# Fourteen batched field pairs instead of ten in a pairwise-interaction kernel, with the transposes placed nearer to their use

## The chip, the cores and the metric

The kernel runs on 1 core of one Trainium2 chip. The metric is the device time of one execution in microseconds (us). Everything is float32.

## The reference

512 examples have 40 categorical fields; each field looks up a row of 64 numbers in its own table. For each of the 780 pairs of fields there is a 64x64 matrix, and the pair's number is a bilinear form. A three-layer tower follows.

```python
e = jnp.stack([tbl_0[ids[:, 0]], ..., tbl_39[ids[:, 39]]], axis=1)   # 512, 40, 64
vi, vj = x[:, i_idx, :], x[:, j_idx, :]                              # 780 pairs i < j
viW = jnp.einsum('bpd,pde->bpe', vi, W)
z = jnp.einsum('bpe,bpe->bp', viW, vj)                               # 512, 780
h = jnp.concatenate([z, dense_ctx], axis=1)                          # 512, 796
h = jnp.maximum(h @ W_top1 + b_top1, 0.0)
h = jnp.maximum(h @ W_top2 + b_top2, 0.0)
y = h @ W_top3
```

## The kernel before, in words

Fields are taken two at a time: **field pair** k holds fields 2k and 2k+1, and the pairs come from k = 19 down to 0. Their place in that order is u = 19 - k; below, f7 means the field pair with u = 7.

A field pair passes through three engines. POOL (GpSimd) gathers its table rows with 8 indirect DMAs (`gather`, L320). PE (TensorE) turns them with four 128x128 transposes into the one PSUM bank `ps_e` (`transpose_fields`, L501). ACT (ScalarE) copies that bank into `E`, a ring of six in SBUF (`copy_fields`, L349), and then issues four DMAs (L356) that place a rearranged copy in `E4`; u = 18 and 19 have no such DMAs. The first four field pairs are made in other ways at the start.

The bilinear forms are computed in two ways.

- A **group** g is a field pair k against one quad M of four later fields (or the pairs inside a quad, M = None). It takes two **steps**. In each, PE writes two matmuls into one of three double banks of `ps_t` (`products`, L539), and DVE (VectorE) multiplies the 128x1024 result by `E` or `E4` into the ring `prod` (`multiply`, L447). Two groups are a couple. PE then sums over the partitions by matmuls with ones into `ps_z` (`reduce_two`, L561), six groups behind the products: 8 matmuls for a couple, or 4 where POOL has added the two halves beforehand (`add_halves`, L327, the groups in `ADDED`). Each chunk of 16 groups fills `ps_z` once, and DVE copies it to `z`.
- A **batched unit** B is a field pair k against the last eight fields, with the batch on the partitions. It takes four steps, one for each 128 examples: PE makes two matmuls (`batched_products`, L522), DVE multiplies by `wide_rows` into one of six buffers of the ring `batched` (`multiply_batched`, L461), and ACT sums it over 64 columns at a time, by 16 ACTIVATEs with an accumulator (`sum_batched`, L372), into `zt`. Here one call of `sum_batched` is called a **sum**; four sums belong to a batched unit, and they are numbered s1, s2, ... in order. A batched unit has no `reduce_two`.

Every engine works strictly through its own list. The lists all come from one generator, `order()`, which says where the transposes ("fields"), the groups and the batched units stand. `ahead(u)` is how many groups before its first use a field pair stands, and `BATCHED`, `BATCHED_FROM` and `BATCHED_EVERY` choose the batched pairs and their places. On ACT the four sums of a batched unit enter the list `left`, and some of the groups take one sum out of it.

The waits that matter here: PE starts step s when the product of step s - 3 is there. DVE's batched step number i (four per unit) waits until i - 5 sums are done, because of the six buffers:

```python
if at >= B_RING:
    dve.wait_ge(batched_summed, at - B_RING + 1)
```

PE's transposes into `ps_e` wait for ACT's previous copy, and groups that use a field pair wait for its copy (`e_copied`). POOL gathers f(u) only when f(u - 4) is transposed.

At the end PE turns `zt` into rows of `z` (L593), and the tower follows: L586 the first layer, L621 the second, L627 the last. The share of the first layer that needs the bank `ps_e` waits for ACT's copy of the first turned part of `zt` (L389), which stands in ACT's list behind the loop.

Weights come by one 256 KB DMA for each couple or batched unit (L289), eight ahead.

Of the kernel before, what the change touches and what calls it, by code (L numbers as in the profile page):

```python
# [25 lines left out]
PER_CHUNK = 16  # L26
# [2 lines left out]
CODE_RING = 7  # L29
G_RING = 4  # L30
E_RING = 6
W_RING = 8
P_RING = 8
B_RING = 6
STEPS = 3
LAG = 7
GATHER_LEAD = 12
PARAMS_AT = 12


# [2 lines left out]

BATCHED = (12, 10, 8, 7, 6, 5, 4, 3, 2, 1)
BATCHED_FROM, BATCHED_EVERY = 7, (13, 3)


def pair(i, j):  # L50
# [3 lines left out]
def plan_groups():  # L54
# [3 lines left out]
    for k in reversed(range(KP)):  # L58
        groups += [(k, M) for M in range(k // 2 + 1, QUADS - (WIDE // 4 if k in BATCHED else 0))]
        if k % 2 == 0:  # L60
# [6 lines left out]
NG = len(GROUPS)  # L67
NC = NG // 2
NB = len(BATCHED)
NU = NC + NB  # L70
CHUNKS = NG // PER_CHUNK
B_PAIRS = 2 * WIDE * NB
B_REST = B_PAIRS - P
ALL_CHUNKS = CHUNKS + 2
DENSE_AT = B_REST


ADDED_COUPLES = (12, 13, 15, 18, 20, 21, 23, 25, 26, 27, 28, 30, 32, 33, 34, 35, 36, 37, 38)
ADDED = [n for n in range(NG) if n // 2 in ADDED_COUPLES]


def arrival(k):
    return KP - 1 - k
# [10 lines left out]


def ahead(u):
    return 1 if u < 8 else 4


SPLIT_FIRST = (0, 2, 3, 1)  # L100
# [12 lines left out]
def order():  # L113

    u = j = units = 0
    for n in range(NG):
        while u < KP and first_group(u) - ahead(u) <= n:
            yield "fields", u
            u += 1
        yield "group", n  # L120
        if n in WIDE_AFTER:
            yield "rows", WIDE_AFTER.index(n)
        units += n % 2
        if n % 2 and j < NB and arrival(BATCHED[j]) < u and units >= (
                BATCHED_FROM + BATCHED_EVERY[0] * j // BATCHED_EVERY[1]):
            yield "batched", j
            j += 1
            units += 1
# [11 lines left out]
def last_step(u):  # L140

    k = KP - 1 - u
    return max([FIRST_STEP["group", n] + 1 for n in range(NG) for ks in pairs_of(n) if k in ks]
               + [FIRST_STEP["batched", j] + 3 for j in range(NB) if BATCHED[j] == k])

# [6 lines left out]
def tower_kernel(nc, w_units, ids, ids_by_field, tables, dense, w1, b1, w2, b2, w3, out):  # L152
    with ExitStack() as ctx:
# [20 lines left out]
        E4 = sb("E4", [P, QUADS - 1, 2, BATCH])  # L174
        w_sb = sb("w_sb", [P, W_RING, BLOCKS * P])
        prod = sb("prod", [P, P_RING, 2, 2, BATCH])
# [4 lines left out]
        small, at = {}, 0  # L181
        for f in looked_up:
            used, c = splits[f]
# [47 lines left out]
        e4_placed = [sem(f"e4_placed{u}") for u in range(KP)]  # L231
        w_loaded = [sem(f"w_loaded{i}") for i in range(W_RING)]
        step_done = sem("step_done")
        product_ready = sem("product_ready")
        halves_added = sem("halves_added")
        two_reduced = sem("two_reduced")
# [31 lines left out]
        def _(sp):  # L268
# [17 lines left out]
            def load_weights(m):  # L286
                if m >= W_RING:
                    sp.wait_ge(step_done, BLOCKS * (m - W_RING + 1))
                sp.dma_start(w_sb[:, m % W_RING, :], w_units[m]).then_inc(w_loaded[m % W_RING], 16)  # L289

            for m in range(W_RING):
                load_weights(m)
# [10 lines left out]
        def _(pool):  # L303
# [27 lines left out]
            for n in range(NG):  # L331
                while u < KP and first_group(u) <= n + GATHER_LEAD:
                    gather(u)
# [4 lines left out]
        @block.scalar  # L338
        def _(act):
            def copy_fields(u):  # L340
                k = KP - 1 - u
                if u < LOOKED_UP:
                    act.wait_ge(code_used, sum(len(codes_of) for codes_of in code_list[:u + 1]))
                else:
                    act.wait_ge(transposed, u - LOOKED_UP + 1)
                if u >= E_RING:
                    act.wait_ge(product_ready, last_step(u - E_RING) + 1)
                    act.wait_ge(e4_placed[u - E_RING], 64)
                act.activation(E[:, slot_of(k), :], e_bank[u], ACT.Copy).then_inc(e_copied, 1)  # L349
                if k < 2:  # L350
                    return
                act.wait_ge(e_copied, place(u) + 1)
                for f in range(2):
                    for h in range(2):
                        to, of = (2 * (k % 2) + f) * HALF, f * DIM + h * HALF
                        act.dma_start(E4[to:to + HALF, k // 2 - 1, h, :], E[of:of + HALF, slot_of(k), :]).then_inc(  # L356
                            e4_placed[u], 16)

            def copy_rows(u):
                at = (KP - 1 - u - WIDE_K) * 2 * DIM  # L360
                act.wait_ge(rows_turned, u + 1)
                act.activation(wide_rows[:, :, at:at + 2 * DIM], ps_e[:].rearrange("p (b n) -> p b n", b=BT),
                               ACT.Copy).then_inc(rows_copied, 1)

            def sum_batched(j, b):

                act.wait_ge(product_ready, FIRST_STEP["batched", j] + b + 1)
                for i in range(2):
                    for f in range(WIDE):
                        at = (2 * j + i) * WIDE + f  # L370
                        products = batched[:, (BT * j + b) % B_RING, i, f, :]
                        last = act.activation(products, products, ACT.Copy, accum_out=zt[:, b, at:at + 1])  # L372
                last.then_inc(batched_summed, 1)

            for u in SPLIT_FIRST:
                copy_fields(u)
            left = []
            for kind, at in order():
                if kind == "fields" and at >= FIRST:
                    copy_fields(at)  # L380
                elif kind == "rows":
                    copy_rows(at)
                elif kind == "batched":
                    left += [(at, b) for b in range(BT)]
                elif kind == "group" and left and at % 7 in (0, 2, 3, 5):
                    sum_batched(*left.pop(0))
            assert len(left) <= (B_REST // (2 * WIDE)) * BT
            act.wait_ge(zt_turned, 1)
            act.activation(z[:, CHUNKS, :], turn_bank[0], ACT.Copy).then_inc(zt_copied, 1)  # L389
            for j, b in left:  # L390
                sum_batched(j, b)
            act.wait_ge(zt_turned, 2)
            act.activation(z[0:B_REST, CHUNKS + 1, :], turn_bank[1][0:B_REST, :], ACT.Copy).then_inc(zt_copied, 1)  # L393
            act.wait_ge(params_loaded, 16 * (ALL_CHUNKS + 5))
            for m in range(H1 // P):
                act.wait_ge(h1_summed, m + 1)
                act.activation(h1[:, m, :], h1_bank[m], ACT.Relu, bias=b1_sb[:, m:m + 1]).then_inc(h1_ready, 1)
            for m in range(H2 // P):
                act.wait_ge(h2_summed, m + 1)
                act.activation(h2[:, m, :], h2_bank[m], ACT.Relu, bias=b2_sb[:, m:m + 1]).then_inc(h2_ready, 1)  # L400
            act.wait_ge(y_summed, 1)
            act.activation(y_sb[:], y_bank[0:1, :], ACT.Copy).then_inc(y_ready, 1)

        @block.vector
        def _(dve):
# [58 lines left out]
                                      ALU.mult).then_inc(product_ready, 1)  # L464

            def copy_z(c):
                dve.wait_ge(two_reduced, PER_CHUNK // 2 * (c + 1))
                dve.tensor_copy(z[:, c, :], ps_z[:]).then_inc(z_copied, 1)  # L468

            for kind, at in order():  # L470
                if kind == "batched":
                    multiply_batched(at)
                elif kind == "group":
                    multiply(at)
                    if at > LAG and at % 2 == 1 and (at - LAG + 2) % PER_CHUNK == 0:
                        copy_z((at - LAG) // PER_CHUNK)
            copy_z(CHUNKS - 1)

        @block.tensor
        def _(pe):  # L480
# [62 lines left out]
            def reduce_two(n):  # L543
                c, q = divmod(n // 2, PER_CHUNK // 2)
                if c >= 1 and q == 0:
                    pe.wait_ge(z_copied, c)
                for g in (n, n + 1):
                    pe.wait_ge(product_ready, FIRST_STEP["group", g] + 2)
                    if g in ADDED:
                        pe.wait_ge(halves_added, ADDED.index(g) + 1)  # L550
                for s in range(2):
                    for g in (n, n + 1):
                        if s == 1 and g in ADDED:
                            continue
                        if GROUPS[g][1] is None:
                            ones = halves[:, 30 - 4 * q - 2 * s:62 - 4 * q - 2 * s]
                        else:
                            ones = quads[:, 28 - 4 * q:60 - 4 * q]
                        for j in range(2):
                            to = 32 * (2 * (g % 2) + j)  # L560
                            last = pe.matmul(ps_z[to:to + 32, :], ones, prod[:, g % P_RING, s, j, :],  # L561
                                             start=(q == 0 and s == 0),
                                             stop=(q == PER_CHUNK // 2 - 1 and (s == 1 or g in ADDED)))
                last.then_inc(two_reduced, 1)

            pe.wait_ge(ident_ready, 1)
# [145 lines left out]
```

## Time and profile before

| | |
|---|---|
| median of 3 runs | 350.28 us (350.03 to 350.73) |
| the profiled execution, its own time | 350.38 us |
| its span in the trace | 348.4 us |
| PE busy | 320.4 us (92%) |
| DVE busy | 250.3 us (72%) |
| POOL busy | 228.4 us (66%) |
| ACT busy | 174.0 us (50%) |
| mean granted clock of TensorE | 0.976 |

The shares are of the span. A program's matmul appears twice in the trace (float32 takes two instructions), so a couple's 8 product matmuls are a row "x16". Matmuls overlap in the records; the time that a block takes is read from the start of one block to the start of the next, or from the chain of waits.

### The profile page before, as it was taken

What the parts mean: (1) busy time and instruction counts of PE and PEld (TensorE: products, weight loads), DVE (VectorE), ACT (ScalarE), POOL (GpSimd) and SP (SyncE); (2) the same over time, 40 slices, a digit from 0 to 9 for tenths busy, and PEclk for the clock granted to TensorE, in tenths of its full rate; (3) what the DMA queues carried; (4) which work ended last, traced back from release to release, by engine and by line L of the source; (5) the groups of instructions that cost most, each with busy time, mean ns of one, the idle gap of its engine ahead of it and who ended that gap; (6) DMA issues with size and microseconds to landing.
All of it is one profiled execution on the core that took longest, in us unless ns stands there. A gap on an engine that the chain in (4) does not pass through costs nothing.

```text
span 348.4 us, 5290 instructions
## 1 busy us (share of the span) xinstructions
PE 320.4 (92%) x1528; PEld 112.4 (32%) x1528; DVE 250.3 (72%) x252; ACT 174.0 (50%) x1312; POOL 228.4 (66%) x192
## 2 busy tenths in 40 slices
PE   0699898529999999999999999999999999999997
PEld 0133432113333333333333333333333333344432
DVE  2385696506887989799899899999998999900000
ACT  1001210000198572876947958795934999190032
POOL 6777777777777734898778884799773994700000
PEclk9999999958999999999999999999999999999969
DMA  6843453323333324933323242322221000000000
GB/s 166 250 149 94 118 131 90 79 49 87 103 95 96 88 77 131 304 83 80 101 67 87 72 109 62 84 68 64 69 66 49 0 3 0 3 0 0 0 0 0
DMA packets 17862, 27.63 MB, mean 79 GB/s; under 512 B 4901, under 2 KB 5029, under 8 KB 17834
## 3 DMA queue, kind: packets, MB, share of 16 engines
q1 hardware_dynamic: 9770, 17.86, 17.8%
q0 software_dynamic: 4608, 4.73, 6.8%
q10 hardware_dynamic: 3456, 4.72, 4.5%
q8 instruction: 12, 0.20, 0.2%
q14 instruction: 16, 0.13, 0.1%
HBM read 22.57 MB, written 0.00 MB: 65 GB/s over the span
## 4 chain that ended last, share of the span: by engine, by line
PE 73%; POOL 16%; issue 6%; DVE 3%; DMA 1%; ACT 0%; DVEq 0%
PE ps_t L539 36%; PE ps_z L561 15%; POOL rows L320 11%; PE ps_t L522 10%; PE ps_t L586 6%; POOL wide_rows L320 5%; PE ps_t L621 3%; DVE prod L447 3%; PE ps_e L501 2%; PE ps_e L586 2%; DMA rows<-in_tbl,ids_sb 1%; DMA ids_sb<-in_ids_t 1%; PE ps_t L627 1%; DVE batched L461 0%; ACT z L393 0%
## 5 line engine op out<-in xcount | busy, mean ns | idle before, releaser
L447 DVE TENSOR_TENSOR prod<-ps_t,E 128x1024 f32<-128x1024 f32 x160 | 184.7, 1217 | 35.6 <-PE ps_t L539 32.0
L372 ACT ACTIVATE batched<-batched 128x64 f32<-128x64 f32 x640 | 152.9, 241 | 23.6 <-DVE prod L447 21.1
L539 PE MATMUL ps_t<-E,w_sb 64*128 64x512 f32 x640 | 156.1, 617 | 1.0 <-DVE prod L447 0.2
L320 POOL DMA_INDIRECT rows<-in_tbl,ids_sb x128 | 121.7, 951 | 38.1 <-issue 37.6
L372 ACT ACTIVATION_READ_ACCUMULATOR batched<-batched 128x1 f32 x640 | 120.0, 188 | 0.0
L327 POOL TENSOR_TENSOR prod<-prod 128x1024 f32<-128x1024 f32 x38 | 89.0, 2371 | 30.0 <-DVE prod L447 29.9
L539 PEld LDWEIGHTS ps_t<-E,w_sb 64*128 64x128 f32 x640 | 55.9, 187 | 90.7 <-issue 60.9
L349 ACT ACTIVATE E<-ps_e 128x512 f32<-128x512 f32 x18 | 10.7, 597 | 102.4 <-PE ps_e L501 79.6
L561 PE MATMUL ps_z<-prod,quads 128*32 128x512 f32 x408 | 58.4, 600 | 0.0
L461 DVE TENSOR_TENSOR batched<-ps_t,wide_rows 128x1024 f32<-128x1024 f32 x40 | 46.2, 1218 | 5.7 <-PE ps_t L522 5.7
L522 PE MATMUL ps_t<-w_sb,E 64*128 64x512 f32 x160 | 37.3, 604 | 0.2 <-DVE batched L461 0.2
L425 DVE TENSOR_SCALAR prod<-prod,first_row_f 125x512 f32<-125x512 int32 x38 | 16.7, 500 | 12.8 <-PE ps_e L490 6.4
L490 PE MATMUL ps_e<-prod 125*64 125x512 f32 x40 | 13.4, 768 | 11.3 <-DVE prod L425 9.5
L561 PEld LDWEIGHTS ps_z<-prod,quads 128*32 128x32 f32 x408 | 11.1, 108 | 35.7 <-issue 20.4
L501 PE MATMUL ps_e<-ident,rows 128*128 128x128 f32 x64 | 10.9, 295 | 12.6 <-DMA rows<-in_tbl,ids_sb 11.8
L522 PEld LDWEIGHTS ps_t<-w_sb,E 64*128 64x128 f32 x160 | 14.2, 186 | 23.4 <-issue 15.7
L320 POOL DMA_INDIRECT wide_rows<-in_tbl,ids_sb x16 | 16.7, 1044 | 5.6 <-issue 4.6
L586 PE MATMUL ps_t<-z,w_sb 128*128 128x512 f32 (+1 forms) x42 | 19.9, 623 | 0.0
L561 PE MATMUL ps_z<-prod,halves 128*32 128x512 f32 x80 | 17.2, 598 | 0.0
L501 PEld LDWEIGHTS ps_e<-ident,rows 128*128 128x128 f32 x64 | 7.0, 145 | 24.1 <-DMA rows<-in_tbl,ids_sb 14.5
L586 PEld LDWEIGHTS ps_t<-z,w_sb 128*128 128x128 f32 (+1 forms) x42 | 7.9, 193 | 10.9 <-issue 10.9
L468 DVE COPY z<-ps_z 128x512 f32<-128x512 f32 x5 | 3.4, 683 | 10.3 <-PE ps_z L561 10.3
(41 smaller groups left out, 61.2 us busy)
## 6 DMA issues: line engine op xcount, KB each, us to landing
w_sb<-in_w_units SPq DMA_DIRECT2D x50, 256.0 KB, 2.8
E<-E ACTq DMA_DIRECT2D x72, 64.0 KB, 2.6
rows<-in_tbl,ids_sb POOLq DMA_INDIRECT x128
w_sb<-in_w SPq DMA_DIRECT2D x7, 256.0 KB
prod<-in_ids_by_field SPq DMA_DIRECT2D x2, 512.0 KB, 9.1
prod<-in_tbl SPq DMA_DIRECT2D x3, 312.5 KB
w_sb<-in_w SPq DMA_DIRECT2D x1, 512.0 KB
wide_rows<-in_tbl,ids_sb POOLq DMA_INDIRECT x16, 4.8
```

Source lines behind the costliest of these rows:

```text
L320: pool.indirect_dma_start(rows_of(u, b)[:, f * DIM:(f + 1) * DIM], None, tables[2 * k + f], bass.IndirectOffsetOnAxis(ap=ids_sb[:, col:col ...
L327: pool.tensor_tensor(prod[:, n % P_RING, 0, :, :], prod[:, n % P_RING, 0, :, :], prod[:, n % P_RING, 1, :, :], ALU.add).then_inc(halves_ad ...
L372: last = act.activation(products, products, ACT.Copy, accum_out=zt[:, b, at:at + 1])
L425: dve.tensor_scalar(codes[0:used, j % CODE_RING, :], ids_wide[0:used, i, :], float(c), first_row_f[0:used, i:i + 1], ALU.subtract, ALU.is_ ...
L447: dve.tensor_tensor(prod[:, n % P_RING, s, :, :], ps_t[:, step % STEPS, :, :], multiplier, ALU.mult).then_inc(product_ready, 1)
L461: dve.tensor_tensor(batched[:, at % B_RING, :, :, :].rearrange("p i f n -> p i (f n)"), ps_t[:, step % STEPS, :, :], wide_rows[:, b, None, ...
L490: pe.matmul(e_bank[u][half:half + DIM, :], small[f][:, c, :], codes[0:splits[f][0], j % CODE_RING, :], start=(c == 0), stop=(c == splits[f ...
L501: last = pe.transpose(e_bank[u][:, b * P:(b + 1) * P], rows_of(u, b), ident[:])
L522: last = pe.matmul(ps_t[:, step % STEPS, i, :], E[at:at + DIM, slot_of(k), b * P:(b + 1) * P], w_sb[at:at + DIM, m % W_RING, :], start=Tru ...
L539: last = pe.matmul(ps_t[:, step % STEPS, j, :], w_sb[at:at + DIM, m % W_RING, col:col + P], E[at:at + DIM, slot_of(pairs_of(n)[s][j]), :], ...
L561: last = pe.matmul(ps_z[to:to + 32, :], ones, prod[:, g % P_RING, s, j, :], start=(q == 0 and s == 0), stop=(q == PER_CHUNK // 2 - 1 and ( ...
L586: last = pe.matmul(h1_bank[m], w1_sb[0:used, c, m * P:(m + 1) * P], z[0:used, c, :], start=(c == 0), stop=(c == ALL_CHUNKS - 1))
```

## The change

There are 14 batched units (k = 14, 12, 11, ..., 0) instead of 10. Each takes two groups away, so there are 72 groups instead of 80, and 50 units in all as before: 36 couples and 14 batched units, instead of 40 and 10. Their places are written out in `BATCHED_AT`, counted in units. 38 groups are still halved by POOL. The transposes stand 1 group ahead (u < 12) or 2 groups, instead of 1 (u < 8) or 4. POOL gathers 14 groups ahead instead of 12. The ring of weights has 6 places instead of 8. On ACT every group takes out a sum while any is left, instead of four groups in seven. `zt` has 224 columns instead of 160, so that the second part turned at the end has 96 rows instead of 32.

```diff
-W_RING = 8
+W_RING = 6
-GATHER_LEAD = 12
+GATHER_LEAD = 14
...
-BATCHED = (12, 10, 8, 7, 6, 5, 4, 3, 2, 1)
-BATCHED_FROM, BATCHED_EVERY = 7, (13, 3)
+BATCHED = (14, 12, 11, 10, 9, 8, 7, 6, 5, 4, 3, 2, 1, 0)
+BATCHED_AT = (4, 6, 9, 11, 14, 17, 21, 24, 28, 31, 35, 38, 42, 45)
...
-CHUNKS = NG // PER_CHUNK
+CHUNKS = -(-NG // PER_CHUNK)
...
-ADDED_COUPLES = (12, 13, 15, 18, 20, 21, 23, 25, 26, 27, 28, 30, 32, 33, 34, 35, 36, 37, 38)
+ADDED_COUPLES = (12, 13, 15, 17, 18, 19, 20, 22, 23, 24, 25, 26, 27, 29, 30, 31, 32, 33, 34)
...
 def ahead(u):
-    return 1 if u < 8 else 4
+    return 1 if u < 12 else 2
...
-        if n % 2 and j < NB and arrival(BATCHED[j]) < u and units >= (
-                BATCHED_FROM + BATCHED_EVERY[0] * j // BATCHED_EVERY[1]):
+        if n % 2 and j < NB and arrival(BATCHED[j]) < u and units >= BATCHED_AT[j]:
             yield "batched", j
...
-                elif kind == "group" and left and at % 7 in (0, 2, 3, 5):
+                elif kind == "group" and left:
                     sum_batched(*left.pop(0))
...
-                dve.wait_ge(two_reduced, PER_CHUNK // 2 * (c + 1))
+                dve.wait_ge(two_reduced, min(PER_CHUNK // 2 * (c + 1), NC))
...
-                                             stop=(q == PER_CHUNK // 2 - 1 and (s == 1 or g in ADDED)))
+                                             stop=((q == PER_CHUNK // 2 - 1 or n == NG - 2)
+                                                   and (s == 1 or g in ADDED)))
```

With the change the middle of the program reads as follows (sums in brackets where ACT's list has them, B0 the first batched unit): g7, B0, g8 [s1], f7, g9 [s2], B1, g10 [s3], f8, g11 [s4], g12 [s5], f9, g13 [s6], B2, g14 [s7], g15 [s8], B3, f10, g16 to g18 [s9 to s11], f11, g19 [s12], B4, g20, g21 [s13, s14], f12, g22, g23 [s15, s16], B5, g24, g25 [s17, s18], f13, and so on; later f14 stands behind s23, f15 behind s28, f16 behind s34, f17 behind s40, f18 behind s45 and f19 behind s50 of 56.

**ACT's list, from the copy of f8 on.** L349 (after: L348) is the copy of a field pair, L356 (L355) its four DMAs, L372 (L371) the sums, 16 ACTIVATEs each. Before:

```order
L349 ACTIVATE E<-ps_e 128x512
L356 DMA E<-E 32x512 x4
L349 ACTIVATE E<-ps_e 128x512
L356 DMA E<-E 32x512 x4
L372 ACTIVATE batched,zt<-batched 128x64 x32
L349 ACTIVATE E<-ps_e 128x512
L356 DMA E<-E 32x512 x4
L372 ACTIVATE batched,zt<-batched 128x64 x48
L349 ACTIVATE E<-ps_e 128x512
L356 DMA E<-E 32x512 x4
```

Now, from the same copy of f8 on:

```order
L348 ACTIVATE E<-ps_e 128x512
L355 DMA E<-E 32x512 x4
L371 ACTIVATE batched,zt<-batched 128x64 x32
L348 ACTIVATE E<-ps_e 128x512
L355 DMA E<-E 32x512 x4
L371 ACTIVATE batched,zt<-batched 128x64 x48
L348 ACTIVATE E<-ps_e 128x512
L355 DMA E<-E 32x512 x4
L371 ACTIVATE batched,zt<-batched 128x64 x48
L348 ACTIVATE E<-ps_e 128x512
L355 DMA E<-E 32x512 x4
```

Sums now stand between the copies of f8 and f9, where none stood, and three instead of two between f9 and f10; by f11 ACT's list has 11 sums behind it instead of 5.

**PE's list, from the transposes of f12 (L501, after: L500) to those of f13.** L539 (L538) are a group's products, 4 matmuls each, L522 (L521) a batched unit, L561 (L560) `reduce_two`. Before:

```order
L501 MATMUL ps_e<-ident,rows 128x128 x4
L539 MATMUL ps_t<-E,w_sb 128x512 x8
L561 MATMUL ps_z<-prod,halves 32x512 x2
L561 MATMUL ps_z<-prod,quads 32x512 x2
L561 MATMUL ps_z<-prod,halves 32x512 x2
L561 MATMUL ps_z<-prod,quads 32x512 x2
L539 MATMUL ps_t<-E,w_sb 128x512 x8
L561 MATMUL ps_z<-prod,quads 32x512 x8
L501 MATMUL ps_e<-ident,rows 128x128 x4
```

Now:

```order
L500 MATMUL ps_e<-ident,rows 128x128 x4
L538 MATMUL ps_t<-E,w_sb 128x512 x8
L560 MATMUL ps_z<-prod,halves 32x512 x2
L560 MATMUL ps_z<-prod,quads 32x512 x2
L560 MATMUL ps_z<-prod,halves 32x512 x2
L560 MATMUL ps_z<-prod,quads 32x512 x2
L521 MATMUL ps_t<-w_sb,E 128x512 x8
L538 MATMUL ps_t<-E,w_sb 128x512 x8
L560 MATMUL ps_z<-prod,quads 32x512 x8
L500 MATMUL ps_e<-ident,rows 128x128 x4
```

A batched unit (B5) now stands between the two, so f13 can be turned only when B5 and the couple behind it are through.

## Rows read from the trace of the kernel before

**Rows 1.** The page: busy time of each engine; PE, ACT, granted clock in 40 slices.

```profile
PE 320.4 (92%) x1528; PEld 112.4 (32%) x1528; DVE 250.3 (72%) x252; ACT 174.0 (50%) x1312; POOL 228.4 (66%) x192
...
PEclk9999999958999999999999999999999999999969
```

**Rows 2.** The chain that ended last, in order of time: start us, us, what.

```profile
73.91 2.37 DMA rows<-in_tbl,ids_sb
76.32 1.12 PE ps_e L501 x4
77.44 3.31 PE ps_t L539 x8
80.75 1.85 PE ps_z L561 x16
82.60 3.63 PE ps_t L539 x16
...
91.72 0.59 PE ps_e L501 x4
...
150.98 1.00 PE ps_z L561 x8
...
289.15 2.17 PE ps_t L539 x8
291.42 2.17 PE ps_t L539 x8
...
304.70 0.59 PE ps_e L593 x4
...
318.83 5.15 PE ps_e L586 x12
```

**Rows 3.** Busy time by stretch, between f8's arrival and the loop's end.

```profile
76.30:302.90 226.60, 225.63 (x1180) 78.04 (x1184) 204.86 (x181) 153.25 (x1228) 171.21 (x125) 0.99 0.29 79
```

**Rows 4.** PE in order of time, around the arrivals of f6, f7 and f8.

```profile
56.98 0.66 PE L501 MATMUL ps_e<-ident,rows 128*128 128x128 f32 x4 [1.18 <-DMA rows<-in_tbl,ids_sb]
...
66.45 0.66 PE L501 MATMUL ps_e<-ident,rows 128*128 128x128 f32 x4 [1.41 <-DMA rows<-in_tbl,ids_sb]
76.32 1.12 PE L501 MATMUL ps_e<-ident,rows 128*128 128x128 f32 x4 [9.21 <-DMA rows<-in_tbl,ids_sb]
```

**Rows 5.** POOL in order of time: two of the 80 gathers in a row.

```profile
70.17 0.94 POOL L320 DMA_INDIRECT rows<-in_tbl,ids_sb  x1 [0.30 <-issue]
71.41 0.95 POOL L320 DMA_INDIRECT rows<-in_tbl,ids_sb  x1 [0.30 <-issue]
```

**Rows 6.** ACT in order of time, two sums (the first 16 ACTIVATEs start 95.46) and a copy.

```profile
95.46 0.26 ACT L372 ACTIVATE batched<-batched 128x64 f32<-128x64 f32 x1 [2.52 <-DVE prod L447]
...
103.12 0.58 ACT L349 ACTIVATE E<-ps_e 128x512 f32<-128x512 f32 x1
103.73 2.44 ACTq L356 DMA_DIRECT2D E<-E  x4
106.22 0.26 ACT L372 ACTIVATE batched<-batched 128x64 f32<-128x64 f32 x1 [2.52 <-issue]
...
117.61 0.18 ACT L372 ACTIVATION_READ_ACCUMULATOR batched<-batched 128x1 f32 x1
```

**Rows 7.** DVE in order of time, twelve steps in a row.

```profile
42.49 13.67 DVE L447 TENSOR_TENSOR prod<-ps_t,E 128x1024 f32<-128x1024 f32 x12 [1.85 <-DMA E<-E]
```

**Rows 8.** Groups of instructions: DVE's steps, and the two halves of ACT's sums.

```profile
L447 DVE TENSOR_TENSOR prod<-ps_t,E 128x1024 f32<-128x1024 f32 x160 | 184.7, 1217 | 35.6 <-PE ps_t L539 32.0 <-DMA E<-E 1.9 <-issue 1.4
L372 ACT ACTIVATE batched<-batched 128x64 f32<-128x64 f32 x640 | 152.9, 241 | 23.6 <-DVE prod L447 21.1 <-issue 2.5
L372 ACT ACTIVATION_READ_ACCUMULATOR batched<-batched 128x1 f32 x640 | 120.0, 188 | 0.0
```

**Rows 9.** Stretches after PE's last work at 67.1: PE busy first, granted clock third from right.

```profile
66.00:68.00 2.00, 0.66 (x4) 0.42 (x4) 0.66 (x1) 0.60 (x1) 1.39 (x3) 1.00 0.07 16
68.00:70.00 2.00, 0.00 (x0) 0.00 (x0) 0.00 (x0) 0.00 (x0) 1.56 (x2) 0.99 0.42 96
70.00:72.00 2.00, 0.00 (x0) 0.00 (x0) 0.00 (x0) 0.00 (x0) 1.53 (x2) 0.50 0.40 97
...
80.00:81.00 1.00, 1.00 (x8) 0.16 (x8) 0.99 (x2) 0.00 (x0) 0.85 (x1) 0.89 0.52 141
```

**Rows 10.** DMA issues on the page: the weights, us from issue to landing.

```profile
w_sb<-in_w_units SPq DMA_DIRECT2D x50, 256.0 KB, 2.8
```

## The prediction

> **What bounds the kernel now.** I read the page first: PE is busy 92% of the span, ACT 50% [rows 1]. Then the chain of waits: it runs over POOL's gathers until f8's rows land, and from 76.32 almost only over PE [rows 2]. Between there and the end of the loop PE is busy 225.6 of 226.6 us, DVE 204.9, ACT 153.3 [rows 3]. So the kernel has two parts: a front paced by gathers, 1.248 us each, 10.0 us for a field pair [rows 5], and a loop paced by PE.
>
> PE's prices, from the chain [rows 2]: a couple's products or a batched unit 3.63 us (a group 1.82), a full `reduce_two` 1.85, a halved one 1.00, four transposes 0.59. After a batched unit a couple takes 2.17 + 2.17 = 4.34, 0.7 more, since DVE's steps come every 1.14 us (13.67 over 12) and PE's every 0.91 [rows 7]; a DVE step by itself is 1.22 [rows 8].
>
> ACT's prices: two sums from 95.46 to 103.12 are 3.83 each, three from 106.22 to about 117.8 are 3.86. I take 3.86. A copy with its DMAs takes 3.10 (103.12 to 106.22), in which ACT sums nothing [rows 6]. A copy without DMAs is 0.6, as the ACTIVATE alone.
>
> **The change on PE.** Four couples become four batched units. Their products cost the same; four full reductions go, 4 x 1.85 = 7.4 us. Also, before f8 there are now two batched units (7.3 us) in place of one couple's tail, so PE is no longer waiting at 76.3. It would wait for f9 instead, 10.0 us later, at 86.3. From f9 on the work is that of before from f8 on, less 0.59 (f8), less ten groups (18.2), plus two batched units (7.3), less five full reductions (9.25): 20.8 less. 10.0 later with 20.8 less work gives -10.8; the slow clock at f8 is gone too (1.12 + 3.31 against 0.59 + 1.82, 2.0 us [rows 2]). **By PE alone the time would be 350.4 - 12.8 = 337.6.**
>
> **The change on ACT.** 16 more sums, 56 in all. ACT's list is serial: 56 x 3.86 = 216.2, copies of f7 to f17 11 x 3.10 = 34.1, f18 and f19 1.2, together 251.5 us behind the first sum's start. That start: f6 lands at 56.98 [rows 4]; now g6 and g7 are behind it. PE will have idled some 7 us there, so I charge the slow clock: transposes 1.12, a group 3.31, a group 1.82, the reduction 1.85, B0's first step 0.91, DVE 1.22 and 0.1 between: 67.3. ACT therefore ends its sums at 318.8 at the earliest, without one wait. Behind them are its copy 0.6 and, from 318.83 to the end, 29.6 us of tail, plus 2.0 outside the span: **351 us is a floor** (349 with the first clock at full). ACT, half idle before, takes away all the gain by itself.
>
> It costs more than the floor, because ACT's lag is passed on through the ring of six. The fourth step of B(j) waits for s(4j - 2): that of B5 for s18. And the transposes stand only one or two groups ahead, so where f(u) comes soon behind B(j), ACT comes to its copy while PE is still held by that very sum. Call T the end of that sum.
>
> - f12 and f13 stand right behind it. From T: DVE 1.25, PE one step 0.91, the next waits for DVE's product (2.4) and ends at 3.4, reduction 1.85, transposes 0.59: ACT waits 5.8 us, twice.
> - f11: the same plus a group (1.82), less s11 (3.86): 3.7. f10: B3 is in between, 9.4 less two sums: 1.7.
> - Before, none of this exists: sums stand four groups in seven and the transposes four groups ahead.
>
> Together 17.0 us. From f14 on the transposes are done before ACT comes (s23, s28 and so on, each one or more sums behind T). Then f17: ACT starts its copy at 67.3 + 40 x 3.86 + 10 x 3.10 + 17.0 = 269.7, while PE has finished B10 at about 264. PE waits; g50 starts at 270.4. From there PE has 22 groups 40.0, three batched units 10.9, reductions 10 x 1.00 + 1.85 = 11.9, two transposes 1.2, 3 x 0.7 behind batched units, and a wait for f18's copy, 2.2 (ACT has five sums before it): 68.3. The loop, with the reduction that stands before `zt` is turned, ends at 338.7. Before it ended at 304.70 [rows 2]; the tail is the same list. That is +34.0: 350.4 + 34.0 = 384.4.
>
> **The clock.** In the trace PE's last work ends at 67.1, and from 70.0 the granted clock is 0.50 (1.2 GHz); it comes back at about 80, and the first 2.4 us of work cost 4.4 [rows 2, 9]. While the ring holds DVE, PE does one step of 0.91 every 3.86 us, so it will be slow at each T too. It lies on the path in the four waits of ACT: 0 to 4 x 2.0 us. I take 6, since these gaps are as long as the one in the row. At f17 the loss takes the place of the wait for f18. The sum is 390.4, I say **390 us**, slower.
>
> The Trainium skill says the same of the clock (TensorE: Matmul & The Clock Gate, HAM oscillation): a kernel whose PE waits between bursts pays the transition each time and not once. Read so, each of the 14 rounds could pay, and only those where PE lies on the path count in the sum.
>
> **Costed at nothing.** The smaller ring of weights: a load lands in 2.8 us [rows 10] and six units are some 30 us ahead; were that cover gone, a miss would show as PE waiting for `w_sb`. The later additions on POOL: 96 gathers end near 144 (f8's last at 73.6, then seven pairs at 10.0), and the first halves (g24) come at about 168. The 96-row turn of `zt`: as many columns as before. POOL's gathers wait for transposes four pairs back, which are still in time (f11 at about 128, needed at 134).
>
> **The rivals.**
>
> - **PE's account holds (faster), 338 us.** It needs ACT out of the way: 56 sums and the copies within some 235 us, that is a sum of at most 3.6 us (238.7 from 67.3 to where the tail would ask for ACT's copy at 306.0, less 35.9, over 56), and of 2.7 us for the ring not to bite at B5, which PE by itself reaches near 135 (67.7 less 18.6 for f7 to f12, over 18). For it: ACT is at 50%. Against: the rows show 3.83 to 3.86 in every stretch. The skill's price points this way (ScalarE: Activation LUTs, What ACT_TABLE_LOAD costs): an ACTIVATE with immediates is 186 ns plus 0.833 ns an element and overlaps the next by 93, so 146 ns for 64 columns, a sum of 2.3 us and 131 us for all. The row has 241 ns from one to the next, since each is followed by an accumulator read of 188 ns that the page does not price; the row decides. So does the rule to shorten the most occupied engine first (Perfetto Trace Analysis, Identifying the Most-Contended Engine). Chance 0.05.
> - **ACT bounds, but never waits for a transpose, 367 us.** Then f17 is copied at 252.7, and the loop ends at 252.7 + 0.7 + 68.3 = 321.7, +17.0: 367.4; with part of the waits up to 376. For it: a copy may find PE further on than I reckon. Against: the orders of f10 to f13 leave no room. Chance 0.16.
> - **The slow clock is held through the waits, 400 to 406 us.** PE's part in the four waits (4.3, 4.3, 6.1 and 7.9 us) doubles in full: +22 on 384.4. For it: PE is busy a quarter of the time there. Chance 0.12.
> - **Both sides cancel, 350 us,** at ACT's floor. Chance 0.01.
>
> **How the numbers follow.** My own case (0.66) runs from 377 (waits of 10 and a clock at full) to 396 (8 more for the clock, 4 for hand-overs of 0.1 us). The range takes in the upper half of the second case and part of the slow clock's: 367 to 400. Two runs of this kernel differ by 0.2%, so "same" is within that. Faster 0.05, same 0.01, slower 0.94.
>
> **What would show it.** ACT's busy share near 60%, its idle time between 67 and 320 below 25 us, and ended by PE's L500 at f10 to f13, some 6 us each at f12 and f13. In the chain ACT's sums (L371) in the place of PE. DVE's L460 waiting for ACT's L371. Granted clock at 0.5 in stretches between 95 and 175. A wait of PE for f17's copy near 264 to 270. The prediction is wrong if ACT's list ends much before 335 us, if PE stays 95% busy from 90 on, or if a sum takes under 3.5 us.

## The result, and the profile after

| | before | after |
|---|---|---|
| median of the runs | 350.5 us (4 runs) | 392.23 us (4 runs, 390.33 to 394.77) |
| ratio, 95% interval | | 1.1195 (1.1126 to 1.1263) |
| span of the profiled execution | 348.4 us | 389.6 us |
| start of the turn of `zt` (L593), which ends the loop | 304.63 us | 349.42 us |
| from there to the end | 43.8 us | 40.2 us |

The change is 12% slower, 390 us were forecast. The loop takes 44.8 us more; the tail, which is what comes behind it, takes 3.6 less.

The page after: the share of each engine, ACT and the granted clock in 40 slices, and the shares of the chain that ended last.

```profile
PE 326.6 (84%) x1464; PEld 113.8 (29%) x1464; DVE 252.2 (65%) x252; ACT 234.7 (60%) x1824; POOL 228.5 (59%) x192
...
ACT  1011110677939091780997979979799999940032
...
PEclk9999978999895896957999799999899999999999
...
ACT 35%; PE 34%; POOL 10%; DVE 7%; ACTq 6%; issue 6%; DMA 1%; DVEq 0%
```

PE has gone from 92% to 84% [rows 1], though it has less to do, and ACT with the DMAs it issues (ACTq) is now 41% of the chain, where it was next to nothing. The waits of after: engine, line, and whom it waited for; in total, times, the longest.

```profile
ACT E L348 <- PE ps_e L500: 45.6, 9, 8.3
...
DVE batched L460 <- ACT batched L371: 36.4, 14, 8.0
...
PE ps_t L538 <- DVE batched L460: 32.6, 13, 7.5
```

These three are the ring: PE waits for DVE's batched step, DVE for ACT's sum, and ACT for PE's transposes. The copies in ACT's list, from f10 on (start, length, what, the idle time ahead of it and what ended it):

```profile
111.63 0.60 ACT L348 ACTIVATE E<-ps_e 128x512 f32<-128x512 f32 x1 [3.51 <-PE ps_e L500]
133.10 0.60 ACT L348 ACTIVATE E<-ps_e 128x512 f32<-128x512 f32 x1 [6.60 <-PE ps_e L500]
155.67 0.60 ACT L348 ACTIVATE E<-ps_e 128x512 f32<-128x512 f32 x1 [7.90 <-PE ps_e L500]
182.55 0.60 ACT L348 ACTIVATE E<-ps_e 128x512 f32<-128x512 f32 x1 [8.33 <-PE ps_e L500]
204.78 0.58 ACT L348 ACTIVATE E<-ps_e 128x512 f32<-128x512 f32 x1
227.35 0.60 ACT L348 ACTIVATE E<-ps_e 128x512 f32<-128x512 f32 x1 [0.26 <-PE ps_e L500]
...
279.43 0.58 ACT L348 ACTIVATE E<-ps_e 128x512 f32<-128x512 f32 x1
```

f10, f11, f12 and f13 wait for PE, f14 does not, f15 hardly, and f17 is copied at 279.43. One turn of the ring in the chain of waits, at f13 (start, length, what):

```profile
158.84 15.40 ACT batched L371 x128
...
174.26 1.24 DVE batched L460
...
175.63 3.79 PE ps_t L538 x8
179.41 2.51 PE ps_z L560 x16
181.93 0.60 PE ps_e L500 x4
...
182.55 0.61 ACT E L348
```

Four sums (s15 to s18, 32 instructions each), DVE's last step of B5, one group, the reduction, the transposes, the copy, each waiting for the one above. Before, a group was 1.8 and the reduction 1.85; here they take 3.79 and 2.51, since the granted clock is 0.50 (1.2 GHz) until it comes back between 180 and 181. The stretches after, in which the third number from the right is the granted clock:

```profile
100.00:180.00 80.00, 55.86 (x232) 17.92 (x236) 43.93 (x38) 48.42 (x392) 36.33 (x38) 0.77 0.30 82
180.00:260.00 80.00, 72.35 (x360) 24.36 (x352) 63.48 (x56) 67.11 (x545) 51.59 (x37) 0.95 0.25 69
...
282.00:349.50 67.50, 66.78 (x335) 22.51 (x332) 65.08 (x58) 62.22 (x514) 45.08 (x22) 0.99 0.13 37
```

Between 100 and 180 PE is busy 70%, between 180 and 260 90%, behind 282 again 99%. So most of the loss is in the first stretch, a smaller part in the second, and PE waits once more, 4.5 us, at f17.

### The profile page after: what moved, and what is told of

It reads as the page before. It is cut to its first block, busy times and chain, and to the rows that moved or that the text cites. A ratio compares the mean times of both kernels' runs of the same rounds, so it can differ in the third digit from the quotient of the medians.

```text
span 389.6 us, 5675 instructions
## 1 busy us (share of the span) xinstructions
PE 326.6 (84%) x1464; PEld 113.8 (29%) x1464; DVE 252.2 (65%) x252; ACT 234.7 (60%) x1824; POOL 228.5 (59%) x192
## 4 chain that ended last, share of the span: by engine, by line
ACT 35%; PE 34%; POOL 10%; DVE 7%; ACTq 6%; issue 6%; DMA 1%; DVEq 0%
ACT batched L371 34%; PE ps_t L538 14%; PE ps_z L560 6%; ACTq L355 6%; POOL rows L319 6%; PE ps_t L586 5%; POOL wide_rows L319 4%; DVE prod L446 4%; PE ps_t L521 3%; DVE batched L460 2%; PE ps_t L621 2%; PE ps_e L586 2%; ACT E L348 2%; PE ps_e L500 2%; DMA rows<-in_tbl,ids_sb 1%
## 5 line engine op out<-in xcount | busy, mean ns | idle before, releaser
L371 ACT ACTIVATE batched<-batched 128x64 f32<-128x64 f32 x896 | 214.0, 241 | 37.4 <-DVE prod L446 15.6
L446 DVE TENSOR_TENSOR prod<-ps_t,E 128x1024 f32<-128x1024 f32 x144 | 167.3, 1217 | 37.2 <-PE ps_t L538 36.3
L538 PE MATMUL ps_t<-E,w_sb 64*128 64x512 f32 x576 | 156.9, 669 | 38.4 <-DVE batched L460 32.6
L371 ACT ACTIVATION_READ_ACCUMULATOR batched<-batched 128x1 f32 x896 | 167.8, 187 | 0.0
L460 DVE TENSOR_TENSOR batched<-ps_t,wide_rows 128x1024 f32<-128x1024 f32 x56 | 65.9, 1219 | 46.8 <-ACT batched L371 36.4
L538 PEld LDWEIGHTS ps_t<-E,w_sb 64*128 64x128 f32 x576 | 54.1, 201 | 126.6 <-issue 82.9
L560 PE MATMUL ps_z<-prod,quads 128*32 128x512 f32 x344 | 52.8, 621 | 0.0
L521 PE MATMUL ps_t<-w_sb,E 64*128 64x512 f32 x224 | 52.4, 604 | 0.4 <-DVE batched L460 0.4
L348 ACT ACTIVATE E<-ps_e 128x512 f32<-128x512 f32 x18 | 10.6, 589 | 68.0 <-PE ps_e L500 45.6
L521 PEld LDWEIGHTS ps_t<-w_sb,E 64*128 64x128 f32 x224 | 19.9, 186 | 33.0 <-issue 22.8
L489 PE MATMUL ps_e<-prod 125*64 125x512 f32 x40 | 12.1, 695 | 12.1 <-DVE prod L424 10.7
L560 PEld LDWEIGHTS ps_z<-prod,quads 128*32 128x32 f32 x344 | 9.8, 113 | 35.5 <-DVE prod L446 19.8
L500 PE MATMUL ps_e<-ident,rows 128*128 128x128 f32 x64 | 10.9, 296 | 9.4 <-DMA rows<-in_tbl,ids_sb 8.6
L560 PE MATMUL ps_z<-prod,halves 128*32 128x512 f32 x80 | 18.0, 621 | 0.0
L500 PEld LDWEIGHTS ps_e<-ident,rows 128*128 128x128 f32 x64 | 7.0, 146 | 21.6 <-DMA rows<-in_tbl,ids_sb 11.1
```

Source lines behind the costliest of these rows:

```text
L446: dve.tensor_tensor(prod[:, n % P_RING, s, :, :], ps_t[:, step % STEPS, :, :], multiplier, ALU.mult).then_inc(product_ready, 1)
L460: dve.tensor_tensor(batched[:, at % B_RING, :, :, :].rearrange("p i f n -> p i (f n)"), ps_t[:, step % STEPS, :, :], wide_rows[:, b, None, ...
L500: last = pe.transpose(e_bank[u][:, b * P:(b + 1) * P], rows_of(u, b), ident[:])
L521: last = pe.matmul(ps_t[:, step % STEPS, i, :], E[at:at + DIM, slot_of(k), b * P:(b + 1) * P], w_sb[at:at + DIM, m % W_RING, :], start=Tru ...
L538: last = pe.matmul(ps_t[:, step % STEPS, j, :], w_sb[at:at + DIM, m % W_RING, col:col + P], E[at:at + DIM, slot_of(pairs_of(n)[s][j]), :], ...
```

## The experiments

In each, the time is set beside runs of the kernel before on the same chip (349.9 to 350.4 us).

**Half of each sum.** In `sum_batched`:

```diff
-                    for f in range(WIDE):
+                    own = (8, 0)[i]
+                    for f in range(own):
...
+                    if own < WIDE:
+                        last = act.activation(zt[:, b, at + own:at + WIDE], batched[:, (BT * j + b) % B_RING, i, own:WIDE, 0], ACT.Copy)
```

> The changed kernel with half of each sum left out: of the 16 ACTIVATEs with accumulator of a sum, 8 stay, and one ACTIVATE of 8 columns stands for the other 8 (it copies the first column of each of those products in place of their sum, so half of the batched pairs are not summed). A sum should take about 8 x 0.241 + 0.2 = 2.1 us instead of 3.85. Theory (ACT's serial list sets the time, through the ring of six and the copies): 2.1 us is below the 2.7 us at which the ring was reckoned to bite, so the time falls to PE's own account, 338 us, at most 345; ACT's waits for transposes at f10 to f13 and the wait of PE for f17's copy are gone. Rival (the transposes one or two groups ahead cost the time by themselves, PE and ACT waiting in turn for each other at each copy, whatever a sum takes): the time stays above 370. Rival (the slow clock and the denser batched units on DVE): above 360.

Measured: 350.18 us (ratio to before 1.0005, 0.9976 to 1.0033). The rivals of 360 and 370 are out: 42 of 392 us go with the length of a sum alone. But 350 is more than the 345 that I allowed, and the copies still wait, at f10 to f13 of this kernel:

```profile
106.63 0.60 ACT L348 ACTIVATE E<-ps_e 128x512 f32<-128x512 f32 x1 [8.69 <-PE ps_e L505]
123.38 0.60 ACT L348 ACTIVATE E<-ps_e 128x512 f32<-128x512 f32 x1 [7.48 <-PE ps_e L505]
138.70 0.60 ACT L348 ACTIVATE E<-ps_e 128x512 f32<-128x512 f32 x1 [6.05 <-PE ps_e L505]
156.06 0.60 ACT L348 ACTIVATE E<-ps_e 128x512 f32<-128x512 f32 x1 [6.05 <-PE ps_e L505]
```

Here that is mostly time ACT has to spare, but the ring also holds DVE for sums that stand behind such a copy: s9 and s10 behind f10, for the last steps of B3.

**Three quarters of each sum.** The same with `own = (8, 4)[i]`.

> As the half sum, but 12 of the 16 ACTIVATEs with accumulator stay and one copies four columns in place of four sums (a quarter of the batched pairs is not summed): a sum of about 12 x 0.241 + 0.2 = 3.1 us. Theory: between the two thresholds reckoned (2.7 for the ring at B5, 3.4 to 3.6 for the end): the ring bites early, from B2 to B5, where PE falls some 10 to 14 us behind its own account, and lets go later, since a round of four sums and a copy (15.5) is then shorter than PE's (15.9): about 350 us, 345 to 358. If the time went with the length of a sum alone (a straight line between the half sum and the whole), it would be 366.

Measured: 364.31 us (1.0387, 1.0297 to 1.0477). This is above the 358 that the two thresholds gave, and near the 366 that I had put down for a time that goes with the length of a sum alone. Against the measured half sum it looks different: the sums are 2.0, 3.0 and 3.8 us long in the three traces, and a straight line between the half and the whole would give 372. So the time does rise more slowly at first, and ACT waits at f10 to f13 (3.8 to 7.7 us) and hardly behind them, as expected; but the thresholds were set too high, and the ring bites at a shorter sum than reckoned.

**Ten buffers.**

```diff
-B_RING = 6
+B_RING = 10
...
-        w1_sb = sb("w1_sb", [P, ALL_CHUNKS, H1])
+        w1_sb = sb("w1_sb", [P, 1, H1])
```

> The changed kernel with ten buffers for the batched products instead of six; to make room, six of the seven blocks of the first layer's weights are left out and the first is used in their place (same number and size of matmuls, 1.5 MB less of loads). Theory: DVE's last step of a batched unit waits for a sum four earlier, so ACT no longer comes to f10 to f13 before PE does: ACT's 26 us of waiting there go, ACT's list itself (56 sums, the copies) stays. f17 is copied at about 253 instead of 279.5, the end follows: 365 us, 360 to 371. If the ring is not what ties them (rival: ACT's list and the places of the transposes do it alone), the time stays at 385 to 392. If nothing but the ring mattered, 338 to 345.

Measured: 365.54 us (1.0422, 1.0328 to 1.0516), as expected to the microsecond. f17's copy is what PE waits for, and its time is the one reckoned, 253:

```profile
253.25 6.71 PE L538 MATMUL ps_t<-E,w_sb 64*128 64x512 f32 x16 [5.30 <-ACT E L348]
```

ACT waits for no transpose from f10 on in this trace: its list runs through, and f17 is copied at 252.57. The 42 us thus have two parts. About 27 are the ring of six, with the waits and the slow clock that come of it; 15 are ACT's list as such, in which f17's copy stands behind 40 sums. The parts hold for this order of taking things away: the DMAs below are also worth 27, and the two overlap. The 1.5 MB of loads that this kernel leaves out were not tried alone; neither this trace nor that of the changed kernel names a load of weights as what PE waits for.

**The transposes further ahead from f12 on.**

```diff
-    return 1 if u < 12 else 2
+    return 1 if u < 12 else 4
```

> The changed kernel with the transposes four groups ahead again, as before the change, but only from f12 on (the change has two there). Theory: f12 and f13 now stand in front of the couple behind B4 and B5, and in ACT's list two sums earlier, so PE is through before ACT comes: the waits of 7.9 and 8.3 us at f12 and f13 go; those at f10 (3.4) and f11 (6.6) stay. f17's copy stands two sums earlier in ACT's list, 7.7 us. Together 16 to 24 us of 392: 368 to 376 us. If the places of the transposes do not matter (rival: only the sum of ACT's work does), 388 to 394.

Measured: 383.79 us (1.0942, 1.0819 to 1.1066). A gain of 8, outside the 16 to 24: the places matter, but less. The copies of f12, f13 and f14 in this kernel:

```profile
139.84 0.60 ACT L348 ACTIVATE E<-ps_e 128x512 f32<-128x512 f32 x1 [0.95 <-PE ps_e L500]
167.26 0.60 ACT L348 ACTIVATE E<-ps_e 128x512 f32<-128x512 f32 x1 [8.93 <-PE ps_e L500]
192.91 0.60 ACT L348 ACTIVATE E<-ps_e 128x512 f32<-128x512 f32 x1 [3.33 <-PE ps_e L500]
```

At f12 the wait is nearly gone. At f13 it is not: the two sums that B4's last steps need now stand behind f12's copy, DVE does the last of these steps at 150.73 (147.81 before the edit), and from there PE has two couples, two reductions and B5 ahead of f13, which ACT waits for. f13 is copied 15.3 us earlier than after the change, f14, which waits again, only 11.9. At 252 the same happens once more: DVE's last step of B9 waits for s34, which now stands behind the copy of f16. The loop ends 8.9 us earlier, so 6.4 of the 15.3 are gone. A transpose moved forward takes its copy forward past sums that DVE waits for. I had counted the waits that go and not those that come.

**The DMAs of the copies on SP's queue.** `place_copy` is the body of the four DMAs of L355:

```diff
+                    if at >= SP_FROM and at < KP - 2:
+                        place_copy(sp, at)
...
-                        act.dma_start(E4[to:to + HALF, k // 2 - 1, h, :], E[of:of + HALF, slot_of(k), :]).then_inc(
-                            e4_placed[u], 16)
+                if k >= 2 and u < SP_FROM:
+                    place_copy(act, u)
```

In the changed kernel (`SP_FROM = 7`):

> The changed kernel, with the four DMAs behind each copy of f7 to f17 issued from SP's queue instead of ACT's (SP waits for the copy; weights are six units ahead). ACT then has 56 sums and 13 copies of 0.6 us, 27 us less in its list before f17. Theory (ACT's serial list sets the pace, with its waits for transposes in it): f17 is copied at about 254 instead of 279.5, and the end follows: 367 us, 360 to 373. Rival (those waits only grow by what ACT saves, since PE and ACT wait in turn for each other): 385 or more. Rival (SP's queue holds the weights up): PE waits for w_sb.

Measured: 364.96 us (1.0416, 1.0376 to 1.0456). The 27 us that leave ACT's list leave the time in full. f17 is copied at 254.59, as reckoned, though ACT's waits for transposes at f8 to f13 are 29.1 us here and were 26.3: they grow by 3 and not by what ACT saves. In the kernel before:

> The kernel before, with the DMAs behind the copies of f7 to f17 issued from SP's queue. If ACT sets nothing there (theory), the time stays within 0.5% of before, 348.5 to 352. If the issuing by ACT was a cost on its own (rival), a good part of the 6 us that it brought the twelve batched units shows here too: under 347.

Measured: 349.7 us (0.9985, 0.9972 to 0.9999), 0.5 us less. The same 27 us of ACT are worth 27 in one kernel and next to nothing in the other.

**Half sums and DMAs on SP together.**

> The half sums (half of the batched pairs is not summed) in the changed kernel, now with the DMAs behind the copies of f7 to f17 on SP's queue as well. The half sums alone left 350 us where PE's account gives 338 to 345, and ACT still waited 4 to 9 us at each of f10 to f15. Theory: there the ring held DVE for sums that stand behind a copy and its 2.5 us of DMA issues in ACT's list, so this part goes too: 342 us, 338 to 345. Rival (PE's account was itself too low, by stalls on DVE or arrivals): it stays at 347 to 351.

Measured: 344.75 us (0.984, 0.9787 to 0.9894), at the upper end of what was expected. So part of the 350 of the half sums was the copy's DMAs in ACT's list. What is left above PE's account stays partly open: between 100 and 140 PE idles 4.0 us of 40 in this kernel, and afterwards DVE is busy 91 to 96% while PE is at 99%:

```profile
100.00:140.00 40.00, 35.99 (x188) 12.25 (x180) 29.79 (x27) 19.72 (x156) 30.25 (x33) 0.96 0.45 131
...
260.00:300.00 40.00, 39.55 (x196) 13.02 (x192) 38.55 (x35) 16.93 (x137) 28.07 (x12) 1.00 0.06 21
```

**A sum at every group in the kernel before.**

```diff
-                elif kind == "group" and left and at % 7 in (0, 2, 3, 5):
+                elif kind == "group" and left:
```

> The kernel before the change, with one edit: ACT takes a sum out of its list at every group instead of at four groups in seven (ten batched units, the transposes as before). Theory: with 40 sums ACT is not the bound, 154 us of sums and 34 of copies in 230 us; a sum that stands a little earlier in its list waits for DVE, and copies may be held up by a few us; within 0.5% of before, 348.5 to 351.5 us. If the new places of the sums alone did the harm (rival): over 355.

Measured: 349.81 us (0.9986, 0.9966 to 1.0005). This edit of the change does no harm by itself.

**Twelve batched units, two of them early.**

```diff
-BATCHED = (14, 12, 11, 10, 9, 8, 7, 6, 5, 4, 3, 2, 1, 0)
-BATCHED_AT = (4, 6, 9, 11, 14, 17, 21, 24, 28, 31, 35, 38, 42, 45)
+BATCHED = (14, 12, 10, 9, 8, 7, 6, 5, 4, 3, 2, 1)
+BATCHED_AT = (4, 6, 11, 15, 19, 23, 27, 31, 35, 39, 43, 46)
...
-ADDED_COUPLES = (12, 13, 15, 17, 18, 19, 20, 22, 23, 24, 25, 26, 27, 29, 30, 31, 32, 33, 34)
+ADDED_COUPLES = (12, 13, 15, 17, 18, 19, 21, 22, 24, 25, 26, 27, 29, 30, 31, 32, 34, 35, 36)
...
-    return 1 if u < 12 else 2
+    return 1 if u < 11 else 4
```

> The changed kernel with twelve batched units instead of fourteen, two of them early (units 4 and 6) and the others three couples apart, each right behind a transpose instead of in front of it, and the transposes one group ahead up to f10 and four from f11 on; POOL halves 38 groups as before. ACT: 48 sums and the copies, 185 + 35 us, from 67.3: 288, against a loop that PE ends near 297 by its own account (70 groups 127.4, twelve units 43.6, reductions 50.3, transposes 8.3, slow clock 2, 0.7 behind each batched unit, from 57.0). Theory (ACT's length and the places of the transposes): little waiting, 343 us, 340 to 348, faster than before by 2%. Rival (early batched units always cost, since ACT falls behind there): 352 or more.

Measured: 346.43 us (0.9877, 0.9844 to 0.9911): faster than before, within 340 to 348, by less than the 2% expected. With the DMAs on SP's queue too:

> As the kernel with twelve batched units, with the DMAs behind the copies of f7 to f17 on SP's queue. ACT has 27 us less. Theory: if ACT still holds PE up in places, this takes it away: equal to the twelve without it or up to 4 us faster, 339 to 344 us. Rival (the DMAs now wait behind the weights in SP's queue, and DVE waits for E4): slower than the twelve without it.

Measured: **340.44 us (0.9709, 0.9676 to 0.9742)**, the fastest here, 2.9% under the kernel before. The stretch from 100 to 140, first of the twelve, then of the twelve with the DMAs on SP:

```profile
100.00:140.00 40.00, 36.99 (x186) 13.91 (x188) 30.00 (x27) 23.86 (x185) 26.85 (x29) 0.91 0.52 151
```

```profile
100.00:140.00 40.00, 39.08 (x216) 14.02 (x212) 34.06 (x31) 29.59 (x234) 31.44 (x31) 1.00 0.58 160
```

PE is busy 2.1 us more in this stretch, and at a clock of 1.00 instead of 0.91. It comes from one place, where a couple waits for the copy of f9 (again first without, then with SP):

```profile
102.10 6.04 PE L538 MATMUL ps_t<-E,w_sb 64*128 64x512 f32 x16 [4.19 <-issue]
```

```profile
98.75 3.71 PE L545 MATMUL ps_t<-E,w_sb 64*128 64x512 f32 x16 [0.95 <-issue]
```

The trace names no releaser, but ACT's copy of f9 ends at 102.00 in the one and at 98.66 in the other, 0.1 us ahead of PE. It stands behind the copy of f8, f8's four DMAs (2.44 us) and four sums. PE starts 3.35 us earlier and, after the shorter wait, does the couple in 3.71 instead of 6.04 us, 2.3 less: that is 5.7 together, and the loop ends 5.7 earlier (299.11 against 304.82). So with the early batched units ACT's DMA issues lay on the path at this place, where in the kernel before they were worth 0.5 us at most.

**Fourteen, spaced.** As the twelve with SP, with the fourteen pairs and the halved groups of the change, and:

```diff
+BATCHED_AT = (4, 6, 10, 13, 17, 20, 24, 27, 31, 34, 38, 41, 44, 46)
```

> Fourteen batched units as in the change, but spaced like the twelve (units 4, 6, 10, 13, 17, 20, 24, 27, 31, 34, 38, 41, 44, 46), the transposes one group ahead up to f10 and four from f11 on, and the DMAs on SP's queue. ACT: 56 sums 216 and 13 copies 8, from 67.5: 291.5 at the earliest, against a loop of PE that would end near 295 (two reductions less than the twelve, 3.7 us). Theory (the count of fourteen is not the harm, its crowding and ACT's list are): 336 to 345 us, the middle 340, since ACT and DVE are then both close to their limit. Rival (fourteen is too many for ACT, however placed): over 350.

Measured: 344.74 us (0.9834, 0.9806 to 0.9862). Fourteen can be faster than before. The same fourteen at the change's places, with the same DMAs on SP, took 364.96; the 20 us between them are the places of the batched units and of the transposes together, since both differ. The spaced fourteen with the DMAs in ACT's list were not run. Two units more than twelve still cost 4.3 us.

**Full rows in the last block.** In the kernel before:

```diff
+            dve.memset(z[:, ALL_CHUNKS - 1, :], 0.0).then_inc(last_zeroed, 1)
...
-                    used = DENSE_AT + DENSE if c == ALL_CHUNKS - 1 else P
+                    used = P
```

> The kernel before, whose last block of z has 48 rows, with that block padded by zeros to 128 rows (its four matmuls read all partitions; the result is the same). In the traces the granted clock fell to half in the tail of the kernels with 48 rows (tail 43.8 and 42.1 us from the turn of zt to the end) and did not fall in those with 80 and 112 rows (40.2 in eight traces). If the rows in use are what the clock goes by: tail 40.2, time 347 to 348.5. If it is something else, such as the gaps between stages: tail 42 to 44, time as before, 349.5 to 351.

Measured: 347.61 us (0.9912, 0.9892 to 0.9932), a tail of 40.2 us. A stretch of the tail, of this kernel:

```profile
332.00:336.00 4.00, 4.00 (x11) 1.79 (x10) 0.00 (x0) 2.75 (x4) 0.00 (x0) 1.00 0.00 0
336.00:340.00 4.00, 4.00 (x10) 1.71 (x9) 0.00 (x0) 0.00 (x0) 0.00 (x0) 1.00 0.00 0
```

and of the kernel before:

```profile
332.00:336.00 4.00, 4.00 (x7) 1.31 (x6) 0.00 (x0) 2.21 (x4) 0.00 (x0) 0.60 0.00 0
336.00:340.00 4.00, 4.00 (x7) 1.66 (x6) 0.00 (x0) 0.00 (x0) 0.00 (x0) 0.55 0.00 0
```

## Why the prediction was right

The forecast was 390 us, the measurement 392.2. Step by step:

- **ACT's prices and start.** A sum was put at 3.86 us; s15 to s18 take 15.40, 3.85 each. The first sum was to start at 67.3 and starts at 67.50. The floor of 351 us from ACT's list alone was to exclude a gain. It was taken with the tail of before; with the tail as it is after the change, 3.6 us shorter, it is 347.5, which leaves room for a gain of 0.8%. What excluded a gain is f17's copy, 40 sums deep in the list.
- **The waits for transposes.** 1.7, 3.7, 5.8 and 5.8 us at f10 to f13, and 6 more for the clock, together 23.0. Measured: 3.51, 6.60, 7.90 and 8.33, together 26.3. Each is 1.8 to 2.9 above the figure reckoned at the full clock, and PE's group takes 3.5 to 3.8 us in place of 1.8 in all four: 9 us for the clock in place of the 6 taken. That f14 to f17 would not wait held, but for 0.26 at f15. ACT's idle time between 67 and 320 was to be below 25 us; these waits alone are above it.
- **f17.** PE was to be held until 270.4 plus the clock's 6; g50 starts at 280.11, 3.7 later, nearly all of it the 3.3 above and f15's wait. PE came there later than reckoned, at 275.6 and not at 264, so its own wait was 4.5 us. Ten buffers moved f17's copy to where the list without waits puts it, and the time to 365.5, against the 367 of the rival that leaves the waits out (this 367 has the tail of before in it). From g50 to the turn of `zt` it is 69.3 us, against 68.3.
- **What the forecast did not have.** The tail is 3.6 us shorter, since the clock no longer falls there. It hides that the loop was put 4.7 us too short: that 390 came within 2 us of 392.2 is in part luck, two errors that cancel.
- **PE's own account was too low.** The rival of 338 us had PE's work in it and little of its stalls. With sums of half the length the kernel takes 350, and with the DMAs gone as well 344.75, though the tail's 3.6 us are gained in both. The thresholds taken from it (2.7 and 3.6 us a sum) were too high, as the three-quarter sum showed: 364 where they gave 345 to 358. The forecast did not rest on them.
- **The Trainium skill's price of an ACTIVATE** (ScalarE: Activation LUTs, What ACT_TABLE_LOAD costs) would have made a sum 2.3 us, and with it the change no loss: the half sum, 2.0 us in its trace, gives 350.2. The rows had the accumulator's read in them, and the choice between the two decided whether a loss was forecast.

What was not tried: a larger ring with all the first layer's weights in SBUF, for which there is no room; the fourteen spaced with the DMAs in ACT's list; and the four waits with PE kept at the full clock, so the 9 us of the clock are read from the trace alone.

## What to carry to other kernels

An engine at 50% busy can be the one that a change runs into: before moving work, add up the list of every engine that gets some, from the moment it can start to the moment its last result is asked for, and see whether it fits. Where three engines hand buffers round in a ring (here transposes, products, sums), look at which result stands behind which in the in-order list of the slowest: a copy moved in front of sums that a full ring waits for can give back much of what it gains (6.4 of 15.3 us here). Work taken off an engine (27 us of DMA issues) is worth all of itself where its list is the bound (27), what it takes out of one wait where the list holds the others up at one place (6), and next to nothing where it does not (0.5).

## What the hardware showed unexpectedly

The granted clock in the tail. In the kernel before, PE is busy without a gap from 331.2 to 340 and beyond, and the clock is at half (1.2 GHz) from about 333 to 339.5. It fell while the four matmuls of the last block were running (330.24 to 334.88), which has 48 rows; a gap of 0.7 us, while ACT copied, lay just ahead of them. Three traces with 48 rows (before, a sum at every group, the DMAs on SP) have tails of 43.8, 42.1 and 42.1 us. All those with 80 or 112 rows have 40.2 and no fall, with the same gap. Zeros up to 128 rows, in the kernel before, bring the same 40.2, and 2.6 us less time (0.9912), with as many matmuls and columns as before. What exactly the chip counts is open; that the padding and nothing else in the tail was changed is what the run shows.

In the loop, the clock fell while the ring held PE. After the change it is at half from 102 (PE had no work from 98.5 to 101.9), from 116 (none from 112.7 on), from 147 (PE had done single steps of 1.1 us, with waits of 1 to 3 us between them) and from 167 (a last step of B5, then none from 165.2 on). Between 100 and 180 its mean is 0.77, and it was 1.00 in the same stretch before. The Trainium skill describes this (TensorE: Matmul & The Clock Gate, HAM oscillation: the transition is paid at each burst between waits), and the trace agrees: the four waits of ACT at f10 to f13 are 1.8 to 2.9 us longer each than reckoned at the full clock.
